# Eight of sixteen scan states summed through transposes in all four orders of the scan, with the side matmuls re-ordered on TensorE

## What is computed

```python
def step(h, xs_t):
    d_t, u_t, B_t, C_t = xs_t
    dA = jnp.exp(d_t[..., None] * A)
    h = h * dA + (d_t * u_t)[..., None] * B_t[:, :, None, :]
    y = jnp.einsum('bkdn,bkn->bkd', h, C_t)
    return (h, y)
...
x_dbl = jnp.einsum('bkdl,kcd->bkcl', xs, x_proj_w)
dts, Bs_, Cs_ = jnp.split(x_dbl, [R, R + N], axis=2)
delta = jax.nn.softplus(dts + dt_b[None, :, :, None])
ys = selective_scan(xs, delta, A, Bs_, Cs_, Ds.reshape(K, D_INNER))
ys = ys[:, 0:2] + ys[:, 2:4, :, ::-1]
```

## Time and profile before

| | |
|---|---|
| median of 3 runs | 14691.99 us (14691.73 to 14700.4) |
| profiled execution, its own time | 14691.09 us |
| its span, first to last instruction | 14689.3 us |
| DVE busy | 12970.4 us, 88% |
| PE busy (pipelined, modelled) | 13181.2 us, 90% |
| ACT busy | 11123.1 us, 76% |
| POOL busy | 10326.6 us, 70% |
| granted TensorE clock | 0.991 mean |

### The profile page before, as it was taken

One profiled execution on the slowest core, in us unless ns is written; L12 is line 12 of the kernel. 1 busy time (PEld: TensorE's weight loads), 2 busy tenths in 40 slices (PEclk: granted clock), 3 DMA queues, 4 the chain that ended last, 5 costly groups with the idle time before them and its releaser, 6 DMA issues.

```text
span 14689.3 us, 247142 instructions
## 1 busy us (share of the span) xinstructions
PE 13181.2 (90%) x65256; PEld 8153.8 (56%) x65256; DVE 12970.4 (88%) x13833; ACT 11123.1 (76%) x22914; POOL 10326.6 (70%) x4126
## 2 busy tenths in 40 slices
PE   6888988889888998889988899888998889988899
PEld 4566455664556645566455664556645566455654
DVE  8999689996899978999689996899969999599995
ACT  5888578885788857887578876788767887678875
POOL 6999069980699807998079970899708996099960
PEclk9999999999999999999999999999999999999999
DMA  3443023430343303443033430344303442043420
GB/s 114 129 131 124 25 93 128 130 124 21 97 130 129 119 21 102 130 141 103 21 111 128 140 96 21 116 130 138 91 21 123 131 138 83 21 131 128 138 78 26
DMA packets 907982, 1468.60 MB, mean 100 GB/s; under 512 B 38912, under 2 KB 891904, under 8 KB 893664
## 3 DMA queue, kind: packets, MB, share of 16 engines
q1 hardware_dynamic: 906560, 1452.37, 31.2%
HBM read 1350.07 MB, written 102.17 MB: 99 GB/s over the span
## 4 chain that ended last, share of the span: by engine, by line
PE 33%; issue 24%; POOL 16%; DVE 15%; ACT 7%; DMA 2%; DVEq 1%; ACTq 1%; POOLq 0%; SPq 0%
POOL area L1794 12%; DVE area L1229 9%; PE ps L756 7%; PE ps L1030 5%; PE ps L1042 5%; DVE area L1257 4%; PE ps L743 3%; POOL area L1804 3%; PE ps L734 3%; ACT ps L1554 3%; DMA area<-bc_rows 2%; PE ps L892 2%; ACT area L1523 2%; PE ps L724 2%; PE ps L856 1%
## 5 line engine op out<-in xcount | busy, mean ns | idle before, releaser
L1229 DVE TENSOR_TENSOR_SCAN area<-ps,hst,area 128x384 f32<-128x384 f32 x9216 | 8581.8, 994 | 150.5 <-ACT ps L1554 69.6
L1794 POOL TENSOR_TENSOR area<-area 128x1152 f32<-128x1152 f32 x3072 | 7998.3, 2638 | 62.6 <-POOL area L1779 29.4
L1554 ACT ACTIVATE ps<-area,a_neg 128x384 f32<-128x384 f32 x9216 | 5259.7, 580 | 984.8 <-DVE area L1229 959.2
L756 PE MATMUL ps<-area,ident 128*128 128x384 f32 x11472 | 4127.3, 494 | 441.5 <-POOL area L1804 408.2
L756 PEld LDWEIGHTS ps<-area,ident 128*128 128x128 f32 x11472 | 2050.0, 191 | 1918.6 <-POOL area L1804 449.4
L743 PE MATMUL ps<-ident,area 128*128 128x128 f32 x20736 | 2882.2, 275 | 0.0
L743 PEld LDWEIGHTS ps<-ident,area 128*128 128x128 f32 x20736 | 2604.0, 192 | 50.3 <-ACT area L1523 1.5
L1523 ACT ACTIVATE area<-ps,area 128x384 f32<-128x384 f32 x3456 | 1972.6, 571 | 560.2 <-PE ps L734 559.4
L1714 ACT ACTIVATE area<-ps,t_neg,area 128x768 f32<-128x768 f32 x1728 | 1617.8, 986 | 1001.1 <-PE ps L1030 1001.1
L1774 POOL TENSOR_TENSOR area<-area,ones 128x2304 f32<-128x2304 f32 x16 | 85.2, 5352 | 3103.5 <-ACT area L1483 2980.9
L734 PE MATMUL ps<-ident,area 128*128 128x128 f32 x10368 | 1765.2, 279 | 326.4 <-ACT area L1523 314.0
(11 more groups left out here) (163 smaller groups left out, 9539.6 us busy)
## 6 DMA issues: line engine op xcount, KB each, us to landing
area<-bc_rows SPq DMA_DIRECT2D x1536, 768.0 KB, 6.7
xz<-x_normed SPq DMA_DIRECT2D x144, 288.0 KB, 6.3
area<-in_x SPq DMA_DIRECT2D x18, 1728.0 KB, 10.1
area<-x_padded SPq DMA_DIRECT2D x24, 1250.0 KB, 12.1
z_raw<-z_st SPq DMA_DIRECT2D x144, 192.0 KB, 6.2
area<-z_raw SPq DMA_DIRECT2D x8, 3456.0 KB, 14.9
x_padded<-x_st SPq DMA_DIRECT2D x120, 200.0 KB, 7.8
x_normed<-area SPq DMA_DIRECT2D x9, 1728.0 KB, 8.1
```

Source lines behind the costliest of these rows:

```text
L756: m = e.matmul(ps[:, 5 + j, 0:CH], ident[:], hb[:, i % NH, j], start=i == 0, stop=i == N - 1)
L1229: e.tensor_tensor_scan(rev(hb[:, i % NH, j], k), rev(ps[:, 2 + j, 0:CH], k), rev(dbu[:, i % NH, j], k), hst[:, i, j:j + 1], ALU.mult, ALU. ...
L1554: e.activation(ps[:, 2 + j, 0:CH], dlt[:, par, j], ACT.Exp, scale=a_neg[:, j, k, i:i + 1]).then_inc(da, 1)
L1794: e.tensor_tensor(dbu[:, i % NH], du[:, par], row_b[:, q % 2, i % ROWS:i % ROWS + 1].broadcast_to([128, J, CH]), ALU.mult).then_inc(dbus, 1)
```

## The change

- One plan, `EIGHT`, takes the place of `FIVE` (orders 0 and 1) and `SEVEN` (orders 2 and 3). The turned states become 1, 3, 4, 7, 9, 10, 12, 13. The pool states become 0, 6, 11 (they were 0, 3, 6, 9 in `FIVE` and 0, 6, 9 in `SEVEN`), the dve states 2, 5, 8, 14, 15 (they were 2, 5, 8, 11, 12, 14, 15 and 2, 5, 8, 11, 14, 15). The units stand at states 10 and 12 (they were at 10 and 14, and at 10 and 13).
- With two tiles in a slot, all of the slot's sums, those of pool states too, and the matmul of L817 or L820 stand between the two tiles.
- A unit stands behind its slot's tiles instead of ahead of them.
- ACT computes two base values of semaphore targets once a position instead of at each wait.

The slots of `EIGHT` (state.tile): 2: 1.0 | 3: 1.1 | 4: 1.2, 3.0 | 5: 3.1, 4.0 | 6: 3.2, 4.1 | 7: 4.2 | 8: 7.0 | 9: 7.1 | 10: 7.2, 9.0 | 11: 9.1, 10.0 | 12: 9.2, 10.1 | 13: 10.2, 12.0 | 14: 12.1, 13.0 | 15: 12.2, 13.1 | 16: 13.2. Those of `SEVEN` are the same up to slot 9 and from slot 13 on; its slots 10, 11, 12 hold one tile each (7.2; 10.0; 10.1).

```diff
--- before.py
+++ after.py
@@ -75,9 +75,8 @@
         self.np, self.nd, self.nt, self.ns = len(pool), len(self.dve), len(self.tiles), len(self.order)
 
 
-FIVE = Plan((0, 3, 6, 9), (1, 4, 7, 10, 13), (10, 14))
-SEVEN = Plan((0, 6, 9), (1, 3, 4, 7, 10, 12, 13), (10, 13))
-PLANS = (FIVE, FIVE, SEVEN, SEVEN)
+EIGHT = Plan((0, 6, 11), (1, 3, 4, 7, 9, 10, 12, 13), (10, 12))
+PLANS = (EIGHT,) * K
 assert 0 in PLANS[0].pool and all(p.order[0] == 0 and p.dve[:3] == (2, 5, 8) for p in PLANS)
 
 
@@ -96,6 +95,7 @@
 
 (P_ALL, P_TO), (D_ALL, D_TO), (T_ALL, T_TO), (S_ALL, S_TO) = (counts(n) for n in ("np", "nd", "nt", "ns"))
 LAST = PLANS[-1]
+assert S_ALL % NC == 0 and all(not p.slots[N + 1] and max(map(len, p.slots.values())) < 3 for p in PLANS)
 
 
 def made_p(b, q, n):
@@ -115,7 +115,7 @@
 
 
 def made_s(b, q, n):
-    return b * S_ALL + (LAST.ns + S_TO[q] + n)
+    return b * NC * (S_ALL // NC) + (LAST.ns + S_TO[q] + n)
 
 
 ADD_AT = {5: 0, 8: 1, 11: 2}
@@ -762,21 +762,34 @@
                     if at:
                         turned_sum(q, at - 1)
 
-                def slot(q, m):
+                def slot(q, m, between=None):
 
                     p = plan(q)
-                    for i in p.order:
-                        if p.sum_at[i] == m and i in p.pool:
-                            state_sum(q, i)
+                    sums = [i for i in p.order if p.sum_at[i] == m]
+                    if len(p.slots[m]) < 2:
+                        for i in sums:
+                            if i in p.pool:
+                                state_sum(q, i)
                     for at in p.slots[m][:1]:
                         tile(q, at)
                     if m == N + 1:
                         turned_sum(q, p.nt - 1)
-                    for i in p.order:
-                        if p.sum_at[i] == m and i in p.dve:
+                    for i in sums:
+                        if i in p.dve or len(p.slots[m]) == 2:
                             state_sum(q, i)
+                    if between:
+                        between()
                     for at in p.slots[m][1:]:
                         tile(q, at)
+
+                def add_y(k, c, m):
+                    if m in ADD_AT:
+                        j = ADD_AT[m]
+                        if k == 0:
+                            e.matmul(ps[:, 5 + j, 0:CH], d_diag[:, j], u_v[:, 0, j, ds(pos(k, c), CH)],
+                                     start=False, stop=False)
+                        else:
+                            e.matmul(y_psum(k)[:, j], ident[:], y_chunk(k, c)[:, j], start=False, stop=False)
 
                 def unit(k, h, q, i):
 
@@ -799,8 +812,6 @@
                                 e.wait_ge(ct_cp, b * GM + 3)
                             e.wait_ge(hcs, made_d(b, q, j))
                             delta_tile(*nxt, j, 1, 0 if last else 64)
-                        if k < UK and m in plan(q).units:
-                            unit(k, h, q, plan(q).units.index(m))
                         if m < 2 and last:
                             slot(q - 1, N + m)
                         if m == 3 and not last:
@@ -808,16 +819,11 @@
                             turn_c(1)
                             alone(e)
                             e.wait_ge(ct_cp, b * GM + GM)
-                        slot(q, m)
+                        slot(q, m, lambda: add_y(k, c, m))
+                        if k < UK and m in plan(q).units:
+                            unit(k, h, q, plan(q).units.index(m))
                         if m < 3 and m in LATE_X and not last:
                             x_proj(1, LATE_X[m])
-                        if m in ADD_AT:
-                            j = ADD_AT[m]
-                            if k == 0:
-                                e.matmul(ps[:, 5 + j, 0:CH], d_diag[:, j], u_v[:, 0, j, ds(pos(k, c), CH)],
-                                         start=False, stop=False)
-                            else:
-                                e.matmul(y_psum(k)[:, j], ident[:], y_chunk(k, c)[:, j], start=False, stop=False)
 
                 walk(e, body)
                 q = K * NC - 1
...
                     g = e.snap(b * 24 + (c + k * NC))
                     g16, g48, q = e.snap(g * 16), e.snap(g * 48), k * NC + c
                     h = e.snap(b * UC + (c + k * NC)) if k < UK else None
+                    tiles[q], made[q] = e.snap(made_t(b, q, 0)), e.snap(made_d(b, q, 0))
...
```

More of the change, by code:

```diff
@@ L1494, in scan_phase @@
             def scan_phase(b):
+                tiles, made = {}, {}
                 def hold_state(k, c, i):
@@ L1512, in c_copy @@
                     e.wait_ge(c_in[q % 2], g * 32 + (16 * (q // 2) + 16))
-                    e.wait_ge(hcs, made_d(b, q0, d))
+                    e.wait_ge(hcs, made[q0] + d)
                     e.activation(ps[:, 1, 0:CH], row_c[:, q % 2, i % ROWS], ACT.Copy).then_inc(c_ps, 1)
@@ L1520, in turned_product @@
                     t = c * 3 if k < 2 else (NC - 1) * 3 - c * 3
-                    e.wait_ge(turn_mm, made_t(b, q, at + 1))
-                    e.wait_ge(turn_sum, made_t(b, q, at - 2))
+                    e.wait_ge(turn_mm, tiles[q] + (at + 1))
+                    e.wait_ge(turn_sum, tiles[q] + (at - 2))
                     e.activation(ht[:, at % 3], ps[:, 0, 0:CH], ACT.Copy,
@@ L1540, in store_y @@
                         e.wait_ge(ysum, made_s(b, k * NC + c, plan(k * NC + c).ns))
-                    e.wait_ge(turn_sum, made_t(b, k * NC + c, plan(k * NC + c).nt))
+                    e.wait_ge(turn_sum, tiles[k * NC + c] + plan(k * NC + c).nt)
                     e.activation(y_chunk(k, c)[:, j], y_psum(k)[:, j], ACT.Copy).then_inc(yev, 1)
@@ L1579, in body @@
                             softplus(g + 1, 1 - par, nxt[0], "ln", LN_AT[i], h=h if i == 11 else None,
-                                     c8=made_d(b, q, plan(q).dve.index(8) + 1))
+                                     c8=made[q] + (plan(q).dve.index(8) + 1))
                         if i >= 1:
```

## The result

| | before | after |
|---|---|---|
| median | 14696.19 us | 15339.11 us (15329.92 to 15347.45, 4 runs) |
| ratio, 95% interval | 1 | 1.0437 [1.0419, 1.0455] |
| span of the profiled execution | 14689.3 us | 15335.2 us |
| DVE, ACT, POOL, PE busy | 12970, 11123, 10327, 13181 | 12697, 11553, 10093, 13809 |

The changed kernel is 4.4% slower. All of the span's 646 us lies in the scan phase: from the first scan of an image to its last, summed over the images, 10397 us became 11043, and the rest stayed at 4292. DVE and POOL have 274 and 233 us less work, as the change meant, and the span grew all the same. The windows of one position after the change answer to the earlier trace rows: length first, then each engine's busy time.

What follows compares the result with a forecast made beforehand. POOL in orders 0 and 1 and DVE in orders 2 and 3 were taken as fullest. Position losses of 3.0, 4.0, 3.7 and 1.85 us, together 12.5, times 48 gave 600 us on 14691.1: 15290 us, range 14770 to 15420.

Steps and rivals of the forecast that it cites:

- three places: DVE waits before the delta step of state 11, state 14 and state 15: about 1.3, 1.9 and 2.7 us.
- The first unit: State 10, orders 0 to 2: unit behind both tiles of slot 10 makes state 12 start 1.36 us late.
- The second unit: State 12, orders 0 to 2: exponential behind the unit's copy makes DVE wait 1.9 us (or 1.2) before state 14.
- The sum of state 11: Slot 14, all orders: sum behind tile 12.1's transpose and back-transpose makes scan (15, 0) wait 2.7 us (or 2.0).
- the larger of the two values: Wait before state 15: 2.7 us if ACT is already late, 2.0 if not; 2.7 was taken.
- the loop: Slots 10 to 15: ACT takes 2.81 us per two-tile state against DVE's 2.74, costing 0.1 in the stretch.
- The sum of the parts: Position losses of 3.0, 4.0, 3.7 and 1.85 us in orders 0 to 3, together 12.5, times 48: 600 us.
- Only the sum: Rival: only the sum of state 11 is waited for, units cost nothing; +124 us, 14815; chance 0.08.
- only the units: Rival: only the units are waited for, the sum of state 11 is hidden; +85 us, 14776; chance 0.07.
- Relief counts: Rival: no wait reaches DVE in states 10 to 15, POOL sets 52.08; 400 us less, 14290; chance 0.10.
- No change: Rival: the sum's wait at its smaller value and none at the units; 14680; chance 0.05.

Runs made afterwards that it cites:

- e2: Changed kernel with two of the four matmul passes of each unit left out; 15147.41 us, ratio to before 1.0306.
- e1: Changed kernel with the sum of pool state 11 ahead of slot 14's tiles again; 15120.24 us, ratio to before 1.0287.
- e3: Changed kernel with the units at the head of slots 10 and 12 again, ahead of the tiles; 15195.24 us, ratio to before 1.0338.
- e7: Kernel before with seven turned states in all orders and each unit behind its slot's first tile; 14612.92 us, ratio 0.9941.
- e8: e7 with the third matmul of the added y in slot 3 instead of slot 11; 14572.86 us, ratio 0.9917.
- e5: Changed kernel with the edits of e1 and e3 together; 15000.01 us, ratio to before 1.0204.

## Why the prediction was right

**The forecast.** 15290 us, 14770 to 15420, was given; 15339 came. The mechanism, its three places and their order of size held. The agreement is closer than the terms deserve: the waits were added up as 6.0 where they give 6.06, and a term that was 0.2 too large stands beside two that were some 0.06 too small.

**Positions.** Forecast 57.7, 58.7, 57.7, 55.1; measured 57.66, 58.69, 57.65, 55.22.

**The first unit.** 1.36 us later at state 12 was forecast. Behind the gap of 1.22 lies the overlap with the scan before and a wait for the exponential: delta step to scan is 0.50 instead of 0.44. From scan (11, 2) to scan (12, 0) it is 1.36 more than without the wait, which is the forecast. That the unit stands in this chain is shown by e2.

**The second unit.** Forecast 1.9, measured 1.7 (a gap of 1.61 and the overlap of 0.08). The unit took 1.29 to the next start, not 1.39: the row that I took it from the earlier trace rows had started behind an idle time. The wait in between, before state 13, was forecast at 0.1 and came at 0.17.

**The sum of state 11.** Forecast 2.7, measured 2.8 in order 2 and 2.65 in order 3 (gaps of 2.68 and 2.57). That the larger of the two values holds, because ACT cannot make up a delay among two-tile states, was the choice with the most weight. ACT's loop over one state, from exponential (12, 0) to (13, 0), is 2.79 us in the rows below, against DVE's 2.74. e1 shows that the place of the sum carries 1.2 us of the wait; that the loop is why it is 2.7 and not 2.0 was read from rows and not tried apart.

```profile
2914.97 1.07 ACT L1563 ACTIVATE ps<-area,a_neg 128x384 f32<-128x384 f32 x2
...
2917.76 1.08 ACT L1563 ACTIVATE ps<-area,a_neg 128x384 f32<-128x384 f32 x2
```

**The sum of the parts.** 12.5 us for four positions was forecast and 12.6 came (2.99 + 4.02 + 3.62 + 1.97). Times 48 that is 605 of 646 us. Of the missing 41 us, 38 lie in order 0. I took all its positions at the 54.67 of a window from its middle. But its second and third positions ran at 53.8 before, bound by DVE (busy for all of 53.84) while POOL still had its lead, and lost 3.8 instead of 3.0: 13 us over the eight images. And the first position of an image lost 3.7 to 7.7 us, 5.7 in the mean, not 3.0: 22 us. The windows below show the second image, where it lost 4.7. Windows from first scan to first scan, of the first and second position, before (two lines) and after (two lines):

```profile
1974.61:2034.81 60.20, 50.90 (x242) 33.63 (x242) 57.43 (x76) 44.88 (x103) 56.36 (x22) 0.97 0.47 149
2034.81:2088.65 53.84, 45.38 (x224) 30.59 (x223) 53.84 (x60) 44.83 (x104) 53.60 (x22) 1.00 0.41 125
...
2053.89:2118.80 64.91, 55.22 (x299) 38.59 (x299) 56.00 (x74) 48.07 (x109) 55.41 (x22) 0.97 0.47 145
2118.80:2176.46 57.66, 50.16 (x286) 36.19 (x286) 51.99 (x58) 48.08 (x111) 51.90 (x21) 1.00 0.39 122
```

The first position holds the input projections of the scan (L688) besides. DVE waited 0.69 us there for the logarithm of state 5 (0.69 to 1.11 over the images), a wait that no other position has. TensorE works without a pause from 2071.09 until then, so it may be behind when the first two-tile slots come; this was not tried.

```profile
2079.66 0.56 DVE L1184 SCALAR_TENSOR_TENSOR area<-area,ps 128x384 f32<-128x384 f32 x1 [0.69 <-ACT ps L1477]
```

**The rivals.** "Only the sum" and "only the units" each had half the truth: both waits are there, and e1, e2 and e3 move one without the other. "Relief counts" fell with the gap before state 15. Its 0.8 us does not follow from the rows: by the prediction's own sums the result of the sum stood at +5.51 against +3.53, 2.0 us too late. "No change" asked for a wait of 2.0 before state 15 and none at the units; 2.8 came, and both units were waited for. The Trainium skill's rule of the engine with the highest occupancy ("Perfetto Trace Analysis", section "Identifying the Most-Contended Engine") picks POOL in orders 0 and 1 (54.43 of 54.67 us) and DVE in orders 2 and 3 (52.9 of 54.0 and 53.3). The change relieved both, by 233 and 274 us, and the time rose by 643 us. The Trainium skill, in the section "Optimization Strategy" of that page, says that one should find the gaps on that engine and the semaphore each one waits for. That is how the forecast, e7 and e8 were made.

## What to carry to other kernels

When the fullest engine has gaps, moving work off it can lose time where the chains that end those gaps have no room for what is moved, as here. Write down, for each wait of the full engine, the serial list of instructions between its cause and its end, and see what the change puts into that list. A single bank that two engines pass back and forth makes a loop with a length of its own (2.8 us here for two tiles); where that is as long as the waiting engine's own step (2.74), a delay stays until the stretch ends. The rows fit this, and no run tried it by itself. Place filler work by where the in-order engine is idle, which may differ between variants of the same loop, and not by the number of instructions it has.

## What the runs showed that I had not expected

A row's duration carries what stood before it: a unit's four passes took 1.39 us to the next start behind an idle time and 1.29 in a full stream. The matmul of the added y takes 1.45 us in odd orders and 0.81 in even ones; in the program, it is its input that is read in permuted order there (`y_chunk`), while it writes PSUM straight. Its place decides over a wait of 1.1 us on another engine (e7, e8). And the waits added almost exactly in order 2: 1.20 and 0.72 us apart, 1.93 together (e1, e3, e5).
